# The second router's front inside the attention, and a shared expert with its inner units on the partitions

## The chip, the cores and the metric

One core of a Trainium2 chip runs the kernel. Times are microseconds on the device for one execution; the metric is the median of the runs.

## What is computed

The input is 16 images of 16 x 16 tokens of 256 channels: 4096 tokens. Two layers, each a mixing part and a mixture of experts, with residuals:

```python
x = x + L0_conv(_ln_c(x))                     # spectral mixing, the kernel's first stage
t = t + L0_ffn(_ln_t(t))                      # 8 experts, top 2
x = x + L1_conv(_ln_c(x))                     # 3x3 convolution, column and row attention with gates
t = t + L1_ffn(_ln_t(t))                      # 8 experts, top 2, and a shared one
# in L1_ffn:
logits = x @ w_router.T; probs = softmax(logits); top 2, weights divided by their sum
routed = square(relu(x @ w1[e].T)) @ w2[e].T  # e: the token's two experts
shared = square(relu(x @ ws1.T)) @ ws2.T      # 256 -> 512 -> 256, every token
return shared + routed
```

## The kernel before

The residual stream `x_res` stays in SBUF, 32 tiles of 128 tokens. Stages follow each other: mixing (0 to 85 us of the profile), first router and experts (to 535), the attention (535 to 843.1), the second router's front (to 903.7) and tail (to 940), the second experts (to 1082), the shared expert (to the end). Products are made in fp32r halves: a number is a high half (a copy in fp32r, ScalarE) and a low one (the rest, VectorE, `low_half`), and `product` (L171 to L179) is three matmuls, high x high, high x low and low x high.

**The attention** takes 8 pairs of images as a pipeline. Each engine has a list of calls, written out by hand and run in order, for steps i = -1 (ScalarE: -2) to 7 + DRAIN, DRAIN = 4: a step convolves pair i (18 convolution steps, `convolve`), makes queries, values, scores and softmax of pair i-1, the gates of pair i-2 (`gate_layer`, six small layers of fp32 between TensorE and VectorE's `leaky`), and attends along the rows, multiplies by `end_w` (`finish`) and adds pair i-3 or i-4 to `x_res`. GpSimd gathers two routed rows for each token (`y_in`), VectorE adds them (`add_routed`), sums them (`statistics`, `deviations`), ScalarE takes the root with Ln and Exp (`root`) and normalises; pair 0 is done whole before pair 1, and then the first step begins. The half of the channels from the pooled branch is added by `join`, pair by pair, in the last steps. ScalarE loads a table ahead of each Exp or Ln of another set.

**The router** (L218 to L523) has a front and a tail. The front takes images one by one: `BATCH_NORM_STATS2` of each tile, root and three Newton instructions for 8 tiles together, normalisation (half on VectorE, half on ScalarE), a store of the normalised rows to `h_rows`, four transposes (`bankT`), a copy to `xT`, and 2 fp32 products a tile with `xT` as the stationary operand and 8 columns of weights. In the same loop the second layer's weights (20 pieces of 512 columns) are loaded to a stage of four, and split (`halves`). The tail selects two experts of 8 for each token and builds the slot tables.

**The shared expert** is `mlp(..., experts=False)`: for each tile of 128 tokens, load the rows, turn them (2 transposes, L640), split, project (6 matmuls of 512 columns, L177 to L179), Relu (L720), square (L767), turn (4 transposes, L647), split, project back (12 matmuls of 256 columns), and add it and the two gathered rows of the experts. Each stage has two buffers (`RING` = 2), so tiles overlap; GpSimd gathers the routed rows (L588).

## Time and profile before

| | us |
|---|---|
| runs | 1211.38, 1213.06, 1213.83 (median 1213.06) |
| profiled execution, and its span | 1207.68, 1205.8 |
| PE busy | 1034.9 (86%) |
| PEld busy | 893.0 |
| DVE busy | 628.5 (52%) |
| ACT busy | 528.2 (44%) |
| POOL busy | 266.8 (22%) |
| mean granted TensorE clock | 0.919 of 2.4 GHz |

PE is TensorE's matmuls, PEld its weight loads, DVE is VectorE, ACT ScalarE, POOL GpSimd, and SP (SyncE) issues the DMAs. Busy shares are means over stages with different limits. PEclk is the granted clock of TensorE, 1.00 for 2.4 GHz and 0.50 for 1.2 GHz.

### The profile page before, as it was taken

What the parts mean: (1) busy time and instruction counts of PE and PEld (TensorE: products, weight loads), DVE (VectorE), ACT (ScalarE), POOL (GpSimd) and SP (SyncE); (2) the same over time, 40 slices, a digit from 0 to 9 for tenths busy, and PEclk for the clock granted to TensorE, in tenths of its full rate; (3) what the DMA queues carried; (4) which work ended last, traced back from release to release, by engine and by line L of the source; (5) the groups of instructions that cost most, each with busy time, mean ns of one, the idle gap of its engine ahead of it and who ended that gap; (6) DMA issues with size and microseconds to landing.
All of it is one profiled execution on the core that took longest, in us unless ns stands there. A gap on an engine that the chain in (4) does not pass through costs nothing. (4 is left out here: it accounts for less than half of the span.)

```text
span 1205.8 us, 20734 instructions
## 1 busy us (share of the span) xinstructions
PE 1034.9 (86%) x5905; PEld 893.0 (74%) x5905; DVE 628.5 (52%) x1686; ACT 528.2 (44%) x1333; POOL 266.8 (22%) x274
## 2 busy tenths in 40 slices
PE   6966679999999999962699999985575799989998
PEld 6955568888888888852466666664575799978997
DVE  5488653222222333225456665455758455546887
ACT  6037254444444444423354555330545566653433
POOL 0000012111111111117522000000000544525664
PEclk9999999999999999985799999975555899999999
DMA  9533501111111111126311100000630344434553
GB/s 356 228 122 123 175 27 49 54 56 54 54 53 53 53 53 53 45 102 181 92 53 53 36 1 1 1 35 1 183 131 1 111 140 138 139 114 130 156 151 107
DMA packets 65398, 110.44 MB, mean 92 GB/s; under 512 B 10068, under 2 KB 47590, under 8 KB 64295
## 3 DMA queue, kind: packets, MB, share of 16 engines
q1 hardware_dynamic: 52070, 73.46, 17.4%
q0 software_dynamic: 12960, 35.41, 10.5%
q8 instruction: 56, 0.92, 0.3%
q10 hardware_dynamic: 288, 0.47, 0.1%
q14 instruction: 24, 0.19, 0.0%
HBM read 73.90 MB, written 35.40 MB: 91 GB/s over the span
## 5 line engine op out<-in xcount | busy, mean ns | idle before, releaser
L580 POOL DMA_INDIRECT experts_rows_sb<-h_rows,ids_i x142 | 134.3, 946 | 762.6 <-POOLq L523 435.6
L767 DVE TENSOR_TENSOR experts_a_sb<-experts_a_sb,experts_bankU 128x512 f32<-128x512 f32 x71 | 48.9, 688 | 224.2 <-PE experts_bankU L179 224.2
L720 ACT ACTIVATE experts_a_sb<-experts_bankG 128x512 f32<-128x512 f32 (+1 forms) x142 | 69.7, 491 | 93.3 <-PE experts_bankG L179 91.9
L711 ACT ACTIVATE experts_hT<-experts_bankH 128x256 fp32r<-128x256 f32 x142 | 54.1, 381 | 89.7 <-PE experts_bankH L640 89.7
L733 ACT ACTIVATE experts_y_sb<-experts_bankY 128x256 f32<-128x256 f32 x142 | 54.5, 384 | 85.6 <-PE experts_bankY L176 66.8
L921 POOL DMA_INDIRECT attn_y<-y_rows,pos_i x64 | 65.1, 1018 | 103.5 <-DVE x_res L1263 50.3
L177 PE MATMUL attn_bankC<-attn_padded,attn_w_half 128*128 128x512 f32 x144 | 75.7, 526 | 6.9 <-ACT attn_feat L1156 4.6
L588 POOL DMA_INDIRECT shared_routed_sb<-y_rows,pos_i x64 | 67.2, 1050 | 62.4 <-DVE x_res L790 34.9
L176 PE MATMUL experts_bankY<-down_plain,experts_aT_plain 128*128 x284 | 72.9, 379 | 0.0
L331 PE MATMUL moe_bankT<-konst_sb,xn 128*128 128x128 f32 x128 | 34.8, 431 | 44.3 <-DVE xn L387 44.3
L182 DVE TENSOR_TENSOR experts_aT<-experts_bankA,experts_aT 128x256 fp32r<-128x256 f32 x142 | 59.6, 420 | 24.0 <-ACT experts_aT L728 24.0
L647 PE MATMUL experts_bankA<-konst_sb,experts_a_sb 128*128 128x128 f32 x426 | 69.7, 273 | 0.4 <-DVE experts_aT L182 0.4
L177 PE MATMUL experts_bankG<-gate_high,experts_hT 128*128 x142 | 69.6, 490 | 0.0
L182 DVE TENSOR_TENSOR experts_hT<-experts_bankH,experts_hT 128x256 fp32r<-128x256 f32 x142 | 59.8, 421 | 18.6 <-ACT experts_hT L711 18.6
L640 PE MATMUL experts_bankH<-konst_sb,experts_rows_sb 128*128 128x128 f32 x284 | 55.4, 277 | 16.3 <-issue 14.2
L178 PE MATMUL attn_bankC<-attn_padded,attn_w_half 128*128 128x512 f32 x144 | 62.7, 436 | 0.0
L179 PE MATMUL attn_bankC<-attn_padded,attn_w_half 128*128 128x512 f32 x144 | 62.4, 433 | 0.0
L767 DVE TENSOR_TENSOR experts_a_sb<-experts_a_sb,experts_bankG 128x256 f32<-128x256 f32 x71 | 29.9, 421 | 58.1 <-ACT experts_a_sb L720 57.4
L331 PEld LDWEIGHTS moe_bankT<-konst_sb,xn 128*128 128x128 f32 x128 | 26.0, 240 | 46.0 <-DVE xn L387 29.1
L342 PEld LDWEIGHTS moe_logits<-router_sb,moe_xT 128*128 128x128 f32 x256 | 58.2, 333 | 1.8 <-ACT moe_xT L307 1.8
L640 PEld LDWEIGHTS experts_bankH<-konst_sb,experts_rows_sb 128*128 128x128 f32 x284 | 37.3, 142 | 26.3 <-issue 17.2
L178 PE MATMUL experts_bankG<-gate_low,experts_hT 128*128 x142 | 56.6, 398 | 0.0
(348 smaller groups left out, 2958.8 us busy)
## 6 DMA issues: line engine op xcount, KB each, us to landing
y_rows<-experts_y_sb SPq DMA_DIRECT2D x142, 128.0 KB
h_rows<-xn SPq DMA_DIRECT2D x32, 256.0 KB, 3.7
x_res<-in_x SPq DMA_DIRECT2D x4, 1024.0 KB, 12.0
mix_xT<-in_xt SPq DMA_DIRECT2D x4, 1024.0 KB, 13.9
gate_raw<-in_L_ffn_gate_w SPq DMA_DIRECT2D x1, 4096.0 KB, 13.8
up_raw<-in_L_ffn_up_w SPq DMA_DIRECT2D x1, 4096.0 KB, 23.2
x_rows<-x_res SPq DMA_DIRECT2D x16, 256.0 KB, 2.4
x_res<-x_rows SPq DMA_DIRECT2D x8, 512.0 KB, 3.8
```

What stands on the lines that cost most here:

```text
L176: return nc.tensor.matmul(out, left[0], right[0], start=start, stop=stop)
L177: nc.tensor.matmul(out, left[0], right[0], start=start, stop=False)
L178: nc.tensor.matmul(out, left[0], right[1], start=False, stop=False)
L179: return nc.tensor.matmul(out, left[1], right[0], start=False, stop=stop)
L182: return eng.tensor_tensor(low, whole, high.bitcast(F32), ALU.subtract)
L580: nc.gpsimd.indirect_dma_start(rows[t % DEPTH][:, :], None, h_dram, bass.IndirectOffsetOnAxis(ap=ids_i[:, t:t + 1], axis=0)).then_inc(s_ro ...
L588: nc.gpsimd.indirect_dma_start(routed[u % DEPTH_R][:, :], None, y_dram, bass.IndirectOffsetOnAxis(ap=pos_i[:, j + k * TILES:j + k * TILES ...
L640: last = nc.tensor.transpose(bankH[:, kc * P:(kc + 1) * P], rows[i % DEPTH][:, kc * P:(kc + 1) * P], K("ident"))
L647: last = nc.tensor.transpose(bankA[:, k * P:(k + 1) * P], a_sb[i % RING][:, k * P:(k + 1) * P], K("ident"))
L720: nc.scalar.activation(a_sb[i % RING][:, :], bankG[i % RING][:, 0:hidden], ACT.Silu if gate is not None else ACT.Relu).then_inc(s["act"], 1)
L767: nc.vector.tensor_tensor(a_sb[i % RING][:, :], a_sb[i % RING][:, :], bankU[i % RING][:, 0:hidden], ALU.mult).then_inc(s["a"], 1)
L921: nc.gpsimd.indirect_dma_start(y_in[u % Y_RING][:, :], None, y_dram, bass.IndirectOffsetOnAxis(ap=pos_i[:, j + k * TILES:j + k * TILES + 1 ...
```

## The change

It has four parts. (1) The front of the second router goes into the attention: pair p's statistics run in step p+4, its transposes, copies and logits in step p+5, DRAIN is 5, the logits stay in `logits1`, the turned rows of a pair go from one buffer `xT` to a new `h_turned` in DRAM, and part 0 of the selection runs in the last step. The logits now have the 8 columns of weights as the stationary operand and 256 columns of `xT` moving, and are turned back. The weights' 20 pieces are split in the steps that `SHARES` names. (2) The attention starts with half pairs (`FIRST`, `SECOND`), convolves 12 of pair 0's 18 convolution steps before it turns pair 1, uses one table set for Ln and Exp (`preload_act_table_set`), and adds the branch in two batches (`JOINS`). (3) The second router is `router_tail` alone. (4) `shared` replaces the `mlp` of the shared expert: groups of 4 tiles, 8 in all, whose turned rows are loaded (512 KB) and split; `ws1` is the stationary operand, so the inner units come out on the partitions and nothing is turned; Relu, Square and Copy run on ScalarE.

```diff
+ht_dram = nc.dram_tensor("h_turned", (P, KC * TOKENS), F32, kind="Internal").ap()
...
-    select(dve, chain, 0)
-    counted.append(chain.n)
-front.close()
-if between is not None:
-    between()
+    dve.wait_ge(s["logits"], PARTS[0][1] // HALVES)
+    choice.select(chain, 0, logits_ps[0][:, 0:PARTS[0][1] * E])
...
+def shared(ws1, ws2):
+    GROUP = 4
+    GROUPS = TILES // GROUP
+    KI = IS // P
+    LEAD = KI + 2
+    DEPTH = 8
+    N = GROUP * P
...
+def load(g):
+    if g >= GROUPS:
+        return
+    if g >= RING:
+        sp.wait_ge(s["h_low"], g - RING + 1)
+    sp.dma_start(hT_raw[g % RING][:, :], ht_dram[:, g * KC * N:(g + 1) * KC * N]).then_inc(s_raw[g % RING], 16)
+for g in range(2 * RING):
+    load(g)
+for g in range(GROUPS):
+    load(g + 2 * RING)
+    for t in range(g * GROUP, (g + 1) * GROUP):
+        sp.wait_ge(s["added"], t + 1)
+        sp.dma_start(out[t * P:(t + 1) * P, :], x_tile(t)).then_inc(s["stored"], 16)
+sp.wait_ge(s["stored"], TILES * 16)
...
+def project(c):
+    g, k = c // KI, c % KI
+    if g >= GROUPS:
+        return
+    pe.wait_ge(s["h_low"], g + 1)
+    if g:
+        pe.wait_ge(s["relu"], c - KI + 1)
+    for kc in range(KC):
+        last = product(bankU[k][:, :], [w[:, kc * IS + k * P:kc * IS + (k + 1) * P] for w in ws1],
+                       [x[:, kc * N:(kc + 1) * N] for x in hT[g % RING]], kc == 0, kc == KC - 1)
+    last.then_inc(s["up"], 1)
+def project_back(t):
+    g = t // GROUP
+    pe.wait_ge(s["a_low"], (g + 1) * KI)
+    if t >= GROUP:
+        pe.wait_ge(s["added"], t - GROUP + 1)
+    for k in range(KI):
+        at = k * N + t % GROUP * P
+        last = product(bankY[t % GROUP][:, 0:C], [x[:, at:at + P] for x in aT[g % RING]],
+                       [w[:, k * C:(k + 1) * C] for w in ws2], k == 0, k == KI - 1)
+    last.then_inc(s["down"], 1)
+for c in range(LEAD):
+    project(c)
+for t in range(TILES):
+    project_back(t)
+    project(t + LEAD)
...
+def activate(c):
+    g, k = c // KI, c % KI
+    act.wait_ge(s["up"], c + 1)
+    if g:
+        act.wait_ge(s["a_low"], c - KI + 1)
+    nc.scalar.activation(a[k][:, :], bankU[k][:, :], ACT.Relu).then_inc(s["relu"], 1)
+    act.wait_ge(s["relu"], c + 1)
+    nc.scalar.activation(a[k][:, :], a[k][:, :], ACT.Square).then_inc(s["square"], 1)
+    act.wait_ge(s["square"], c + 1)
+    if g >= RING:
+        act.wait_ge(s["down"], (g - RING + 1) * GROUP)
+    nc.scalar.activation(aT[g % RING][0][:, k * N:(k + 1) * N], a[k][:, :], ACT.Copy).then_inc(s["a_high"], 1)
+high_h(0)
+high_h(1)
+for c in range(GROUPS * KI):
+    activate(c)
+    if c % KI == KI - 1:
+        high_h(c // KI + RING)
...
+def low_a(c):
+    g, k = c // KI, c % KI
+    if g >= GROUPS:
+        return
+    dve.wait_ge(s["a_high"], c + 1)
+    part = slice(k * N, (k + 1) * N)
+    low_half(nc.vector, aT[g % RING][1][:, part], a[k][:, :], aT[g % RING][0][:, part]).then_inc(s["a_low"], 1)
+def add_routed(t):
+    if t >= TILES:
+        return
+    for k in range(2):
+        u = t * 2 + k
+        dve.wait_ge(s_routed[u % DEPTH], (u // DEPTH + 1) * 16)
+        if k:
+            dve.wait_ge(s["sum"], u)
+        nc.vector.scalar_tensor_tensor(out=x_tile(t), in0=routed[u % DEPTH][:, :], scalar=w_top[:, t + k * TILES:t + k * TILES + 1],
+                                       in1=x_tile(t), op0=ALU.mult, op1=ALU.add).then_inc(s["sum"], 1)
+def add_y(t):
+    dve.wait_ge(s["down"], t + 1)
+    dve.wait_ge(s["sum"], t * 2 + 2)
+    nc.vector.tensor_tensor(x_tile(t), x_tile(t), bankY[t % GROUP][:, 0:C], ALU.add).then_inc(s["added"], 1)
+low_h(0)
+low_h(1)
+for c in range(LEAD):
+    low_a(c)
+    if c == KI - 1:
+        low_h(RING)
+add_routed(0)
+for t in range(TILES):
+    add_routed(t + 1)
+    add_y(t)
+    c = t + LEAD
+    low_a(c)
+    if c % KI == KI - 1:
+        low_h(c // KI + RING)
...
+SHARES = {0: 3, 1: 3, 2: 2, 8: 3, 9: 2, 10: 2, 11: 2, 12: 3}
...
+loaded = 0
+for i in range(0, PAIRS + DRAIN):
+    if has(i + 2):
+        sp.wait_ge(s["sum"], (i + 1) * 2 * PT)
+        load_x(i + 2)
+    while loaded < min(share[i].start + len(stage), len(pieces)):
+        halves.load(sp, loaded)
+        loaded = loaded + 1
+    if i in BATCH_AT:
+        b = BATCH_AT.index(i)
...
+    if has(i - 5):
+        width = KC * 512
+        sp.wait_ge(s["f_copied"], 2 * (i - 5) + 2)
+        sp.dma_start(ht_dram[:, (i - 5) * width:(i - 4) * width], xT[:, :]).then_inc(s_turned_out, 16)
+    if has(i - 4):
+        for m in range(2 * (i - 4), 2 * (i - 4) + 2):
+            sp.wait_ge(s["f_xn"], m + 1)
+            sp.dma_start(rows[:, m * HALVES:(m + 1) * HALVES, :],
+                         xn[m % RING][:, :].rearrange("p (h c) -> p h c", c=C)).then_inc(s_stored[m % RING], 16)
+for b in range(RING):
+    sp.wait_ge(s_stored[b], IMAGES // RING * 16)
+sp.wait_ge(s_turned_out, PAIRS * 16)
...
+def turn_rows(p, n):
+    if not has(p):
+        return
+    m = p * 2 + n
+    pe.wait_ge(s["f_xn"], m + 1)
+    pe.wait_ge(s["lows"], min(2 * (p + 5) + 2, IMAGES))
+    if m:
+        pe.wait_ge(s["f_copied"], m)
+    for kc in range(KC):
+        for h in range(HALVES):
+            last = nc.tensor.transpose(bankT[:, (kc * HALVES + h) * P:(kc * HALVES + h + 1) * P],
+                                       xn[n][:, h * C + kc * P:h * C + (kc + 1) * P], K("ident"))
+    last.then_inc(s["f_turned"], 1)
...
+def route(p, n, kc):
+    if not has(p):
+        return
+    pe.wait_ge(s["f_copied"], p * 2 + n + 1)
+    pe.wait_ge(s["feat2"], min(p + 3, PAIRS))
+    if p:
+        pe.wait_ge(s["f_kept"], p)
+    part = slice(n * 256, (n + 1) * 256)
+    last = nc.tensor.matmul(bankX[0:E, part], router1[:, kc * E:(kc + 1) * E], xT[:, kc * 512 + n * 256:kc * 512 + (n + 1) * 256],
+                            start=(kc == 0), stop=(kc == KC - 1))
+    if (n, kc) == (1, KC - 1):
+        last.then_inc(s["f_logits"], 1)
+def turn_logits(p):
+    if not has(p):
+        return
+    pe.wait_ge(s["f_logits_t"], p + 1)
+    for t in range(PT):
+        last = nc.tensor.transpose(bankX[:, t * E:(t + 1) * E], logits_t[:, t * P:(t + 1) * P], K("ident", E)[:, 0:E])
+    last.then_inc(s["f_turned_back"], 1)
...
-for i in range(-1, PAIRS + DRAIN):
+turn(0, 0)
+turn(0, 1)
+convolve(0, 0, 12)
+turn(1, 0)
+convolve(0, 12, STEPS)
+turn(1, 1)
+for i in range(1, PAIRS + DRAIN):
...
+turn_rows(i - 5, 0)
 gate_layer(i - 2, 1)
-convolve(i, 5, 6)
-turn(i + 1, 0)
-convolve(i, 6, 7)
+convolve(i, 5, 7)
+turn_rows(i - 5, 1)
 gate_layer(i - 2, 2)
 convolve(i, 7, 8)
 scores(i - 1, "down")
 convolve(i, 8, 9)
+turn(i + 1, 0)
+route(i - 5, 0, 0)
 gate_layer(i - 2, 3)
 convolve(i, 9, 10)
 scores(i - 1, "along")
 convolve(i, 10, 11)
+route(i - 5, 0, 1)
 gate_layer(i - 2, 4)
+route(i - 5, 1, 0)
 convolve(i, 11, 12)
+turn_values(i - 1)
+route(i - 5, 1, 1)
+convolve(i, 12, 13)
+branch(i)
+gate_layer(i - 2, 5)
+convolve(i, 13, 14)
 turn(i + 1, 1)
-turn_values(i - 1)
-convolve(i, 12, 13)
-gate_layer(i - 2, 5)
-branch(i)
-convolve(i, 13, 14)
 turn_probs(i - 1, "down")
+turn_logits(i - 5)
...
+def roots(p, f, tiles=WHOLE):
+    cols = slice(tiles[0], tiles[-1] + 1)
+    if has(p):
+        act.wait_ge(s["var"], batch(p, tiles) + 1)
+        nc.scalar.activation(m_log[:, cols], m_var[:, cols], ACT.Ln).then_inc(s["log"], 1)
+    if has(f):
+        act.wait_ge(s["f_var"], f + 1)
+        nc.scalar.activation(f_log[:, :], f_var[:, :], ACT.Ln).then_inc(s["f_log"], 1)
+    if has(p):
+        act.wait_ge(s["log"], batch(p, tiles) + 1)
+        nc.scalar.activation(m_rstd[:, cols], m_log[:, cols], ACT.Exp, scale=-0.5).then_inc(s["root"], 1)
+    if has(f):
+        act.wait_ge(s["f_log"], f + 1)
+        nc.scalar.activation(f_rstd[:, :], f_log[:, :], ACT.Exp, scale=-0.5).then_inc(s["f_root"], 1)
...
+def copy_rows(p, n):
+    if not has(p):
+        return
+    act.wait_ge(s["f_turned"], p * 2 + n + 1)
+    if p:
+        act.wait_ge(s["f_logits"], p)
+        act.wait_ge(s_turned_out, p * 16)
+    nc.scalar.activation(xT[:, :].rearrange("p (k x) -> p k x", k=KC)[:, :, n * 256:(n + 1) * 256],
+                         bankT[:, :].rearrange("p (k x) -> p k x", k=KC), ACT.Copy).then_inc(s["f_copied"], 1)
+def copy_logits(p):
+    if not has(p):
+        return
+    act.wait_ge(s["f_logits"], p + 1)
+    nc.scalar.activation(logits_t[:, :], bankX[0:E, :], ACT.Copy).then_inc(s["f_logits_t"], 1)
...
+nc.scalar.preload_act_table_set("natural_log_exp_and_others")
 act.wait_ge(loads["conv"], 16)
 for n in range(W_PARTS):
     nc.scalar.activation(w_half[0][:, w_part(n)], w_raw[:, w_part(n)], ACT.Copy).then_inc(s["w_high"], 1)
-nc.scalar.activation(warm[:, :], K("ones")[:, 0:4], ACT.Ln)
 act.wait_ge(s["border"], 1)
-for i in range(-2, PAIRS + DRAIN):
+for n, half in enumerate((FIRST, SECOND)):
+    roots(0, PAIRS, half)
+    normalise(0, half)
+    high(0, n)
+roots(1, PAIRS)
+normalise(1)
+for i in range(0, PAIRS + DRAIN):
     if i == 1:
         act.wait_ge(loads["attn"], ATTN_LOADS * 16)
     relu(i - 1)
     copy_feat2(i - 3)
     queries(i - 1)
+    copy_rows(i - 5, 0)
+    copy_rows(i - 5, 1)
     high(i + 1, 0)
     exponentials(i - 1, "down")
     exponentials(i - 1, "along")
+    if i > PAIRS + 2:
+        roots(i + 2, i - 4)
+    copy_logits(i - 5)
+    values(i - 1)
+    gate_exp(i - 2)
+    if i <= PAIRS + 2:
+        roots(i + 2, i - 4)
     high(i + 1, 1)
-    values(i - 1)
-    root(i + 2)
-    gate_exp(i - 2)
     copy_along(i - 1)
     copy_gated(i - 2)
     normalise(i + 2)
-    relu_branch(i)
+    for piece in share[i]:
+        halves.high(act, piece)
...
+def normalise_rows(p):
+    if not has(p):
+        return
+    dve.wait_ge(s["f_root"], p + 1)
+    chain(nc.vector.tensor_tensor(f_newton[:, :], f_var[:, :], f_rstd[:, :], ALU.mult))
+    chain(nc.vector.tensor_tensor(f_newton[:, :], f_newton[:, :], f_rstd[:, :], ALU.mult))
+    chain(nc.vector.tensor_scalar(f_newton[:, :], f_newton[:, :], -0.5, 1.5, ALU.mult, ALU.add))
+    chain(nc.vector.tensor_tensor(f_scale[:, :], f_rstd[:, :], f_newton[:, :], ALU.mult))
+    chain(nc.vector.tensor_tensor(f_bias[:, :], f_mean[:, :], f_scale[:, :], ALU.mult))
+    for n in range(2):
+        if p:
+            dve.wait_ge(s["f_turned"], p * 2 + n - 1)
+            dve.wait_ge(s_stored[n], p * 16)
+        for h in range(HALVES):
+            t = n * HALVES + h
+            last = nc.vector.tensor_scalar(xn[n][:, h * C:(h + 1) * C], x_tile(p * PT + t), f_scale[:, t:t + 1], f_bias[:, t:t + 1],
+                                           ALU.mult, ALU.add)
+        last.then_inc(s["f_xn"], 1)
+def keep_logits(p):
+    if not has(p):
+        return
+    dve.wait_ge(s["f_turned_back"], p + 1)
+    last = nc.vector.tensor_copy(logits1[:, p * PT * E:(p + 1) * PT * E], bankX[:, 0:PT * E])
+    last.then_inc(s["f_kept"], 1)
...
-add_routed(0, 0, range(PT))
-for t in range(PT):
-    low_weights(t)
-    add_routed(0, 1, range(t, t + 1))
-statistics(0)
-deviations(0)
+for k in range(2):
+    add_routed(0, k, FIRST)
+statistics(0, FIRST)
+low_weights(0)
+add_routed(0, 0, SECOND[0:1])
+deviations(0, FIRST)
+add_routed(0, 0, SECOND[1:2])
+low_weights(1)
+low_weights(2)
+add_routed(0, 1, SECOND[0:1])
+low_weights(3)
+add_routed(0, 1, SECOND[1:2])
+statistics(0, SECOND)
 lows(0, 0)
+deviations(0, SECOND)
+add_routed(1, 0, WHOLE)
 lows(0, 1)
-for k in range(2):
-    add_routed(1, k, range(PT))
+add_routed(1, 1, WHOLE)
 statistics(1)
 deviations(1)
 tables()
+JOINS = {(4, 0): (0,), (4, 1): (1, 2), (5, 1): (3,), (8, 0): (4,), (8, 1): (5,), (9, 1): (6, 7)}
 for i in range(0, PAIRS + DRAIN):
     sum_rows(i - 2)
     sum_columns(i - 3)
     add(i - 4)
+    if i == PAIRS + DRAIN - 1:
+        choice.select(chain, 0, logits1[:, 0:PARTS[0][1] * E])
     add_routed(i + 2, 0, range(0, PT // 2))
     leaky(i - 2, 0)
+    for p in JOINS.get((i, 0), ()):
+        join(p)
+    row_stats(i - 4, 0)
     add_routed(i + 2, 0, range(PT // 2, PT))
     leaky(i - 2, 1)
-    lows(i + 1, 0)
+    row_stats(i - 4, 1)
     add_routed(i + 2, 1, range(0, PT // 2))
     leaky(i - 2, 2)
+    row_stats(i - 4, 2)
     add_routed(i + 2, 1, range(PT // 2, PT))
-    join(2 * (i - PAIRS))
     maximum(i - 1, "down")
     leaky(i - 2, 3)
+    row_stats(i - 4, 3)
+    lows(i + 1, 0)
     statistics(i + 2)
-    join(2 * (i - PAIRS) + 1)
     maximum(i - 1, "along")
     leaky(i - 2, 4)
+    row_variances(i - 4)
     soften(i - 1, "down")
-    lows(i + 1, 1)
     soften(i - 1, "along")
+    relu_branch(i)
     bound(i - 2)
     copy_down(i - 1)
     sigmoid(i - 2)
+    if i <= PAIRS + 2:
+        keep_logits(i - 5)
     apply_rows(i - 2)
+    lows(i + 1, 1)
     apply_columns(i - 3)
     deviations(i + 2)
+    if i >= PAIRS:
+        normalise_rows(i - 4)
     copy_attended(i - 1)
+    if i < PAIRS:
+        normalise_rows(i - 4)
+    for p in JOINS.get((i, 1), ()):
+        join(p)
+    for piece in share[i]:
+        halves.low(dve, piece)
+    if i > PAIRS + 2:
+        keep_logits(i - 5)
...
-mlp("shared", TILES, IS, ws1, ws2, experts=False, sink=out)
...
+with routing:
+    router_tail("moe1", choice, logits1[:, PARTS[1][0] * E:PARTS[1][1] * E])
+mlp("experts1", SLOT_TILES, I1, up1, down1)
+shared(ws1, ws2)
```

Not shown: `row_stats` and `row_variances` are `BATCH_NORM_STATS2` of one tile, and the small sums from them; `high_h` and `low_h` split a group's h as ScalarE's copy (one instruction of 1024 columns) and VectorE's rest; both `row_` functions run in the step that adds the pair.

## Rows read from the trace of the kernel before

**Rows 1.** Windows by stage: busy us (count) of PE, PEld, DVE, ACT, POOL; PEclk, DMA, GB/s.
```profile
535.00:563.80 28.80, 2.20 (x8) 1.43 (x8) 13.34 (x45) 10.27 (x18) 21.82 (x21) 0.50 0.68 218
563.80:596.50 32.70, 19.24 (x63) 14.32 (x63) 19.52 (x70) 10.81 (x20) 21.13 (x20) 0.76 0.36 109
596.50:792.50 196.00, 190.08 (x929) 129.56 (x929) 109.44 (x325) 92.30 (x250) 22.17 (x24) 0.99 0.09 26
792.50:843.10 50.60, 34.26 (x151) 26.00 (x150) 27.14 (x80) 10.55 (x32) 0.00 (x0) 0.62 0.05 20
843.10:903.70 60.60, 40.85 (x192) 39.74 (x192) 40.19 (x133) 29.68 (x58) 0.00 (x0) 0.50 0.49 156
903.70:940.00 36.30, 18.57 (x76) 16.99 (x76) 25.36 (x79) 17.25 (x66) 3.78 (x4) 0.50 0.05 15
940.00:1082.00 142.00, 137.85 (x1135) 135.75 (x1134) 77.58 (x213) 94.02 (x284) 63.29 (x67) 0.99 0.42 129
1082.00:1205.80 123.80, 114.97 (x768) 103.10 (x768) 94.55 (x192) 44.17 (x96) 67.20 (x64) 0.97 0.47 137
```

**Rows 2.** Timeline of DVE, end of the attention to the selection: start us, busy us.
```profile
841.71 1.42 DVE L1401 TENSOR_TENSOR x_res<-x_res,attn_branches 128x256 f32<-128x256 f32 x4
844.36 0.75 DVE L360 BATCH_NORM_STATS2 stats<-x_res 128x6 f32<-128x256 f32 x2 [1.24 <-PEq L120]
...
903.66 0.23 DVE L256 TENSOR_REDUCE moe_top<-moe_logits 128x8 f32<-128x64 f32 x1 [3.76 <-PEq L407]
```

**Rows 3.** Timeline of PE in one tile of the shared expert.
```profile
1153.13 0.40 PE L177 MATMUL shared_bankG<-ws,shared_hT 128*128 128x512 f32 x1
...
1154.53 0.38 PE L640 MATMUL shared_bankH<-konst_sb,shared_rows_sb 128*128 128x128 f32 x2
1154.74 0.60 PE L647 MATMUL shared_bankA<-konst_sb,shared_a_sb 128*128 128x128 f32 x4
1155.10 0.36 PE L177 MATMUL shared_bankY<-ws,shared_aT 128*128 128x256 f32 x1
...
1156.61 0.40 PE L177 MATMUL shared_bankG<-ws,shared_hT 128*128 128x512 f32 x1
```

**Rows 4.** Groups of instructions by line: busy us, mean ns of one, idle before.
```profile
L588 POOL DMA_INDIRECT shared_routed_sb<-y_rows,pos_i x64 | 67.2, 1050 | 62.4 <-DVE x_res L790 34.9 <-POOLq L535 16.8 <-issue 10.7
L720 ACT ACTIVATE shared_a_sb<-shared_bankG 128x512 f32<-128x512 f32 x32 | 19.1, 598 | 65.1 <-PE shared_bankG L179 62.9 <-issue 2.2
```

**Rows 5.** Timeline of PE in a full step: its final product, an fp32 product.
```profile
736.35 1.16 PE L1072 MATMUL attn_bankS_along<-end_w,attn_gated 128*128 128x128 f32 x8
...
740.29 1.07 PE L965 MATMUL attn_bankQ<-attn_feat,qk_w 128*64 128x512 f32 x2
```

**Rows 6.** Timeline of ACT and PE in one full step of the attention.
```profile
728.75 1.28 ACT L1138 ACT_TABLE_LOAD   x1
...
731.99 0.66 PE L1043 MATMUL attn_bankX<-konst_sb,attn_gated 128*128 128x128 f32 x4 [0.80 <-DVE attn_gated L1373]
```

**Rows 7.** Timeline of PE at the attention's start.
```profile
580.87 1.12 PE L937 MATMUL attn_bankT<-konst_sb,attn_xn 128*128 128x128 f32 x4 [10.19 <-ACT attn_xn L1128]
```

**Rows 8.** Timeline of DVE in the second router's front.
```profile
848.50 0.17 DVE L375 TENSOR_TENSOR newton<-var_eps,rstd 128x8 f32<-128x8 f32 x1
...
849.52 0.73 DVE L387 TENSOR_SCALAR xn<-x_res,rstds,moe_shift 128x256 f32<-128x256 f32 x2
```

**Rows 9.** Timeline of PE: the final products of steps 8 to 11.
```profile
792.97 1.16 PE L1072 MATMUL attn_bankS_along<-end_w,attn_gated 128*128 128x128 f32 x8
...
814.49 1.16 PE L1072 MATMUL attn_bankS_along<-end_w,attn_gated 128*128 128x128 f32 x8
...
828.03 2.08 PE L1072 MATMUL attn_bankS_along<-end_w,attn_gated 128*128 128x128 f32 x8
...
838.99 2.08 PE L1072 MATMUL attn_bankS_along<-end_w,attn_gated 128*128 128x128 f32 x8
```

**Rows 10.** Timeline of PE: a group of transposes in the drain.
```profile
805.99 1.12 PE L1001 MATMUL attn_bankQ<-konst_sb,attn_exp_down 128*128 128x128 f32 x4
```

465 lines of the change are left out of this document (275 added, 190 removed).

## The prediction

> **What bounds the kernel now.** I read the windows by stage first [rows 1]. The attention's steps keep TensorE busy (190 of 196 us at clock 0.99), and so do the second experts (138 of 142 us) and the shared expert (115 of 124 us). Three stretches are bound by chains between engines: the attention's start (535 to 596.5 us), its drain (792.5 to 843.1 us, clock 0.62) and the second router's front (843.1 to 903.7 us, clock 0.50, TensorE and VectorE both two thirds busy). The front is serial: it begins when the last join has ended, and the tail begins after it [rows 2]. The shared expert's token tile was read from the timeline [rows 3]: six products of 512 columns take 1.40 us, the two transposes of h 0.21 us, the four of a 0.36 us, twelve products of 256 columns 1.51 us, 3.48 us in all with no gap. The remaining rows are the prices of what moves and the waits near it.
>
> **The front leaves.** From the last join's end (843.13 us) to the tail's first instruction (903.66 us) lie 60.5 us; the same barrier that now stands between 843.13 and 844.36 us stays [rows 2]. So 59.3 us go, before what comes back.
>
> **What comes back in the full steps (i = 5 to 7).** TensorE gets, for each pair of images, 8 transposes, 4 fp32 products of 256 columns and 4 small transposes of the logits. Four transposes cost 0.36 us [rows 3]; an fp32 product of 512 columns runs in two passes of 1.07 us together [rows 5], so one of 256 about 0.5 us; the small ones I put at 0.1 each (between nothing, hidden, and the 0.09 of a full transpose plus a start). That is 0.7 + 2.0 + 0.5 = 3.2 us a step, and TensorE has no idle time to put it in: a step of 28.3 us (two of them from 736.35 to 792.97 us, [rows 5, 9]) has one gap of 0.8 us [rows 6]. The second group of transposes waits for ScalarE's copy of the first, which stands behind five activations of the queries: 0.7 us more. VectorE gets about 6.5 us a step: 4 statistics (0.35 each, [rows 2]), small sums (0.9), five chained small ones (1.0) and four normalisations (0.35 each, [rows 8]), a join. VectorE is busy 109 of 196 us [rows 1], 16 of 28 us a step, so its share fits, but the normalisations (2.5 us) stand behind the copy of the attended values and in front of the sums of rows and columns, for which the next step's first gate layer waits on TensorE, and behind that layer the queries, values and everything else. The slack there is about 1 us, so 1.9, 1.2 and 0.5 us with the joins, 3.6 in all. Sum for three steps: 3 x 3.9 + 3.6, rounded to +16 us. Bounds: +8 if the VectorE work is hidden, +25 if each added VectorE microsecond after the copy reaches TensorE.
>
> The weight halves (20 pieces of 512 columns, 0.6 us each on ScalarE [rows 4] and, as two 256-column pieces, 0.7 on VectorE [rows 2]) are split over steps 0 to 2 (8 pieces) and 8 to 12 (12). In steps 0 to 2 they stand just ahead of the relu that frees the convolution's bank, 0.6 us each on ScalarE: +5 us (bounds 0 and +8).
>
> **Table loads.** Each step loads two activation tables ahead of the gate's exponential; one load is 1.28 us, and TensorE then waits 0.8 us for the gated values [rows 6]. With logarithm and exponential in one set both loads go: 7 x 0.8, about -5 us (bounds 0 and -6; nothing if the set is not kept). The Trainium skill (ScalarE: Activation LUTs, Table sets: the hidden batching unit) says the same of that set, and under What ACT_TABLE_LOAD costs it adds a drain, 2.66 us a switch. The trace has the next activation right behind the 1.28 us; by the page's figure the loads would be worth twice as much to ScalarE, and the sum would still end at the 0.8 us gaps.
>
> **The attention's start.** Now the gathers of four tiles, two each, must land before the first statistics; the second pair's convolution operands come so late that TensorE waits 10.2 us at 580.87 us [rows 7], and step 1 starts at 596.5 us. The change takes the first half pair's tokens as soon as its own four gathers are in, fills TensorE with 12 of 18 convolution steps before it turns the next pair, and takes its table loads off. Following the queues with the durations of this stretch, the first convolution starts near 559 instead of 563.8 us and step 1 near 584: -12 us. Bounds: 0, if the next gathers set the pace (GpSimd issued gathers for 21.8 of the first 28.8 us, [rows 1]), and -16.
>
> **The drain.** Before, from one final product to the next, steps 8 to 10 take 21.5, 13.5 and 11.0 us, and 4.1 us are left to the end [rows 9]: with what lies ahead of the first, 50.6 us [rows 1]. Now steps 8 to 10 carry the router's work of pairs 3 to 5, and 11 and 12 that of pairs 6 and 7. At half clock four transposes take 0.95 to 1.12 us [rows 10], the four products 4 us, the logits' turn 0.9: nearly 7 us of TensorE a step, laid between gate layers that wait about 0.5 us each on VectorE. I take +5 for step 8 and +4.5 each for 9 and 10. Step 11 grows from 5 to about 11: behind the final product and addition come statistics, roots and normalisation of pair 7 (8 us), while TensorE works through pair 6. Step 12 is new, a bare chain: turn, copy, turn, copy, four products, copy, turn back, copy, with three weight halves in front of the last copy, about 10 us. Sum 14 + 6 + 10 = +30 us. Bounds: +18 (clock 2.4 GHz, the halves hidden) and +45 (each step as long as its VectorE and TensorE work end to end).
>
> **The shared expert.** Six transposes a tile go: 0.57 us x 32 = 18.2 us [rows 3]. TensorE stays the bound if the others fit in 2.91 us: ScalarE runs three dependent 512-column activations of 0.6 us a tile [rows 4] and a quarter of a 1024-column one, 2.1 us, or 2.5 if each hand-over costs 0.15; VectorE about 2.3 (94.6 us over 32 tiles [rows 1], less the 0.7 of the squaring); GpSimd two gathers of 1.05 plus 0.3 between them [rows 4], 2.7 us. The start is some 4 us later (512 KB to load and split instead of 128 KB, four chunks before the first product back), but six projections are done by then, and after the last product one addition stands instead of three. I take -18. Bounds -12 (ScalarE or gathers at 3.1 us a tile) and -20.
>
> **Sum**: -59.3 + 16 + 5 - 5 - 12 + 30 - 18 = -43 us on the profiled execution's 1207.7 us: 1164 us. The median of the runs is 5.4 us above that execution, so 1170 us.
>
> **Rivals.**
> A, the clock. The drain is at half clock because TensorE is idle a third of it [rows 1]; the added work could hold 2.4 GHz. Then its 7 us a step halve, five times 3.5 us, of which about 12 lie on the chain: 1158 us. For it: the drain begins at full clock; against it: the front did much the same work, two thirds busy, at 0.50 throughout [rows 1]. Chance 0.13. The Trainium skill (TensorE: Matmul & The Clock Gate, What's actually happening) ties the clock to how busy the engine has recently been, which speaks for A; what was added is a third transposes, which Part 4: PE-mode transpose says do not count as busy.
> B, the start gains nothing: gathers set its pace. 1182 us. For it: GpSimd's share there; against it: TensorE's long wait ends on normalised rows, not on a gather. 0.14.
> C, the shared expert becomes ScalarE's or GpSimd's: 1176 us. ScalarE was busy only 44 of 124 us, but its work is now chained. 0.07.
> D, the front is moved but not hidden: VectorE becomes the bound of steps 4 to 7 and of the drain, both terms at their upper bounds (+9 and +15). 1194 us. 0.07.
> E, slower than before: one buffer holds the turned rows, and the copy of a pair waits until the store of the pair before has landed; the store waits in SyncE's queue behind weight loads that wait for VectorE. If each of 8 pairs waited over 43/8 = 5.4 us for it, the gain is gone; at 7 us a pair it would be 1170 + 56 = 1226 us. A store of such a size lands in about 4 us after its issue and steps are 11 us or longer, so there is slack. 0.04.
>
> **Chances.** Forecast 0.55. What a measurement of this kernel can tell from no change is about 0.2%. All but E are faster: 0.95, with 0.01 within 0.2% and 0.04 slower. The range takes in A, B, C and the near side of D, and the terms' bounds where only one or two fail together: 1150 to 1192 us.
>
> **What would show it.** Right: no stage between the attention's last step and the router's selection, the tail starting near 878 us (903.7 - 59.3 + 16 + 5 - 5 - 12 + 30); steps 5 to 7 some 4 to 5 us longer; the 10.2 us wait gone; fewer than three table loads in the attention; shared tiles 2.9 us apart with TensorE busy. Wrong: gaps on TensorE in front of the first gate layer above 3 us a step, a drain over 95 us, waits on ScalarE's chain or on gathers in the shared expert, or SyncE holding the turned rows. The numbers fail most easily in the drain, which is worked out from durations, not read.

## The result, and the profile after

The changed kernel took 1196.28 us (median of 4 runs, 1192.82 to 1199.71), the kernel before 1212.22 beside it: ratio 0.9882, 95% interval 0.986 to 0.9905. It is faster, as forecast, but by 16 us instead of 43, and lies above the range of 1150 to 1192 us. Its windows by stage, cut at the same places as before [rows 1]; the columns are the same:

```profile
535.00:601.90 66.90, 23.21 (x70) 15.73 (x70) 34.46 (x125) 16.49 (x37) 39.82 (x40) 0.60 0.50 157
601.90:785.90 184.00, 174.79 (x837) 117.09 (x837) 116.84 (x374) 77.75 (x230) 24.04 (x24) 0.97 0.17 55
785.90:898.70 112.80, 93.50 (x408) 58.22 (x407) 69.90 (x235) 37.86 (x98) 0.00 (x0) 0.74 0.23 80
898.70:935.00 36.30, 18.54 (x76) 17.00 (x76) 25.39 (x79) 16.15 (x65) 3.79 (x4) 0.50 0.05 15
935.00:1078.00 143.00, 139.13 (x1135) 136.62 (x1134) 77.72 (x213) 94.23 (x284) 63.45 (x67) 0.98 0.42 128
1078.00:1197.30 119.30, 99.63 (x576) 87.58 (x576) 69.85 (x136) 65.70 (x104) 65.38 (x64) 0.90 0.47 142
```

The tail starts at 898.7 us where 878 was forecast, and the shared expert takes 119.3 us where some 106 were. Both shortfalls have a place. First the attention's start, timeline of TensorE, with the idle time before an instruction and its releaser in brackets:

```profile
572.92 0.42 PE L180 MATMUL attn_bankC<-attn_padded,attn_w_low 128*128 128x512 f32 x1
...
576.24 0.56 PE L178 MATMUL attn_bankC<-attn_padded,attn_w_high 128*128 128x512 f32 x1 [2.13 <-issue]
578.38 0.59 PE L179 MATMUL attn_bankC<-attn_padded,attn_w_high 128*128 128x512 f32 x1 [1.58 <-issue]
580.48 0.58 PE L180 MATMUL attn_bankC<-attn_padded,attn_w_low 128*128 128x512 f32 x1 [1.51 <-issue]
...
601.93 0.77 PE L178 MATMUL attn_bankC<-attn_padded,attn_w_high 128*128 128x512 f32 x1 [8.73 <-ACT attn_feat L1432]
```

The three matmuls from 576.24 to 580.48 us are of one product, wait for nothing in the program, and begin 2.1 us apart instead of 0.26. In the same microseconds VectorE and ScalarE stand still (timelines of the two):

```profile
576.25 0.41 DVE L183 TENSOR_TENSOR attn_bias_part<-attn_bias_raw,attn_bias_part 2x256 fp32r<-2x256 f32 x1 [7.11 <-issue]
...
589.92 0.66 ACT L1423 ACTIVATE attn_padded<-attn_bankT 128x256 fp32r<-128x256 f32 x2 [20.12 <-remote]
```

VectorE's instruction follows the one before it on its own engine. The transposes for which ScalarE would wait here ended at 572.56 us. I call such a stretch a stall. Two more lie in the shared expert; the first of them, timeline of TensorE:

```profile
1111.34 0.40 PE L179 MATMUL shared_bankU<-shared_hT,ws 128*128 128x512 f32 x1
1112.25 0.40 PE L180 MATMUL shared_bankU<-shared_hT,ws 128*128 128x512 f32 x1 [0.51 <-issue]
1114.34 0.39 PE L178 MATMUL shared_bankU<-shared_hT,ws 128*128 128x512 f32 x1 [1.69 <-issue]
1115.09 0.39 PE L179 MATMUL shared_bankU<-shared_hT,ws 128*128 128x512 f32 x1 [0.36 <-issue]
```

### The profile page after: what moved, and what is told of

It reads as the page before. It is cut to its first block and busy times, and to the rows that moved or that the text cites. A ratio compares the mean times of both kernels' runs of the same rounds, so it can differ in the third digit from the quotient of the medians.

```text
span 1197.3 us, 19835 instructions
## 1 busy us (share of the span) xinstructions
PE 1025.8 (86%) x5686; PEld 858.5 (72%) x5686; DVE 615.7 (51%) x1712; ACT 528.2 (44%) x1328; POOL 264.1 (22%) x274
## 5 line engine op out<-in xcount | busy, mean ns | idle before, releaser
L178 PE MATMUL attn_bankC<-attn_padded,attn_w_high 128*128 128x512 f32 x144 | 76.4, 530 | 19.8 <-ACT attn_feat L1432 14.6
L834 POOL DMA_INDIRECT shared_y<-y_rows,pos_i x64 | 65.4, 1022 | 63.9 <-DVE x_res L943 32.1
L178 PE MATMUL experts_bankG<-gate_high,experts_hT 128*128 x142 | 69.6, 490 | 0.0
L180 PE MATMUL attn_bankC<-attn_padded,attn_w_low 128*128 128x512 f32 x144 | 63.8, 443 | 1.5 <-issue 1.5
L179 PE MATMUL attn_bankC<-attn_padded,attn_w_high 128*128 128x512 f32 x144 | 63.6, 442 | 1.6 <-issue 1.6
L179 PE MATMUL experts_bankG<-gate_low,experts_hT 128*128 x142 | 56.6, 398 | 0.0
L178 PEld LDWEIGHTS attn_bankC<-attn_padded,attn_w_high 128*128 128x128 f32 x144 | 28.7, 199 | 38.3 <-issue 32.9
L180 PE MATMUL experts_bankG<-gate_high,experts_hT 128*128 x142 | 55.7, 392 | 0.0
L180 PE MATMUL experts_bankU<-up_high,experts_hT 128*128 x142 | 55.5, 391 | 0.0
## 6 DMA issues: line engine op xcount, KB each, us to landing
mix_xT<-in_xt SPq DMA_DIRECT2D x4, 1024.0 KB, 14.1
```

Source lines behind the costliest of these rows:

```text
L178: nc.tensor.matmul(out, left[0], right[0], start=start, stop=False)
L179: nc.tensor.matmul(out, left[0], right[1], start=False, stop=False)
L180: return nc.tensor.matmul(out, left[1], right[0], start=False, stop=stop)
L834: nc.gpsimd.indirect_dma_start(routed[u % DEPTH][:, :], None, y_dram, bass.IndirectOffsetOnAxis(ap=pos_i[:, t + k * TILES:t + k * TILES + ...
```

## The experiments

Eighteen more runs, some of them the same kernel again, were made in five more sets; the kernels of a set run on one chip and share the runs of the kernel before. That one took 1199.46 us in set 2 and 1209.64, 1210.71, 1211.72 and 1210.17 in sets 3 to 6, against 1212.22 in the first. So set 2 differs from the others, and ratios are compared within a kind. The chip is not the difference: sets 2 and 6 ran on the same one.

**again** (set 2): the changed kernel, no edit.

> The changed kernel, nothing altered. In its first trace the tail starts at 898.7 us, 20 us later than forecast, and the shared expert takes 119.3 us, 14 longer than forecast. Most of it lies in three stretches where several engines start their instructions one or two microseconds apart with no releaser in the trace: 569 to 590 us in the attention's start, 1110 to 1118 and 1154 to 1158 in the shared expert. Theory 1: these stalls belong to the changed program (its instructions, or the transfers around them): the second trace has them at the same instructions with the same length, and the ratio to the kernel before is again 0.986 to 0.990. Theory 2: they come and go with the execution: the trace has them elsewhere or not at all, step 1 of the attention begins near 584 us instead of 601.9, and the span differs by over 5 us.

Measured: 1166.88 us against 1199.46, ratio 0.9722 (0.9702 to 0.9743). Its windows, cut at the same instructions:

```profile
535.00:582.90 47.90, 19.09 (x71) 14.09 (x71) 33.85 (x123) 16.00 (x37) 36.98 (x36) 0.68 0.64 203
582.90:766.30 183.40, 174.32 (x837) 117.44 (x837) 116.91 (x374) 77.41 (x230) 28.03 (x29) 0.97 0.19 59
766.30:877.80 111.50, 91.97 (x408) 57.64 (x407) 69.97 (x236) 37.73 (x98) 0.00 (x0) 0.75 0.24 81
877.80:914.00 36.20, 18.48 (x76) 16.99 (x76) 25.36 (x79) 16.05 (x65) 3.78 (x4) 0.50 0.05 15
914.00:1057.00 143.00, 139.05 (x1135) 136.62 (x1134) 77.72 (x213) 94.36 (x284) 63.30 (x67) 0.97 0.42 128
1057.00:1162.20 105.20, 92.69 (x576) 83.04 (x576) 70.10 (x136) 66.51 (x104) 67.47 (x64) 0.94 0.53 161
```

Row by row the two traces agree within 1.3 us, except in the first (19.0 us shorter) and the last (14.1 us shorter), where the stalls lie. So it is theory 2: the stalls come and go, by sets. ScalarE's copy that stood 20 us comes 1.6 us after the transposes:

```profile
570.09 0.67 ACT L1423 ACTIVATE attn_padded<-attn_bankT 128x256 fp32r<-128x256 f32 x2 [2.34 <-PE attn_bankT L1154]
```

The two traces differ in a second way. Here is the same wait of TensorE in the changed kernel's first trace and in this one:

```profile
556.97 1.12 PE L1154 MATMUL attn_bankT<-konst_sb,attn_xn 128*128 128x128 f32 x4 [5.91 <-issue]
```
```profile
554.96 1.12 PE L1154 MATMUL attn_bankT<-konst_sb,attn_xn 128*128 128x128 f32 x4 [5.89 <-ACT attn_xn L1397]
```

It is an ordinary wait for ScalarE, and as long in both; the first trace merely names no releaser for it. Counted from the traces, both hold 19835 instructions, but the first holds 9118 records of semaphores being raised and this one 12988. All 20 traces of this case hold 4229 to 4253 of them up to 520 us. Behind that the three traces of set 2 hold 8743 to 9168 more, and the 17 others 4855 to 5749. So "no releaser" is no sign of a stall in a trace of the other sets; a stall is told by instructions that wait for nothing and yet stand apart. And every trace with stalls has lost records too, so the recording itself, or what hinders both, is a rival for their cause. No run tests it: each execution on record was profiled.

**start_old** (set 2) and again in set 6: the start of the kernel before.

```diff
-                convolve(0, 0, 12); turn(1, 0); convolve(0, 12, STEPS); turn(1, 1)
+                convolve(0, 0, 6); turn(1, 0); convolve(0, 6, 12); turn(1, 1); convolve(0, 12, STEPS)
-                for n, half in enumerate((FIRST, SECOND)): ...
+                roots(0, PAIRS); normalise(0); high(0, 0); high(0, 1)
```

> The attention's start of the kernel before (pair 0 whole, its order of gathers, pair 1 turned after 6 and 12 of 18 convolution steps), all else as changed. Theory 1, the new start is worth what I forecast and the stall at 569 to 590 us hides it: with the old start step 1 begins near 596 us less the table loads (3 us), so 593 to 597, some 5 to 8 us earlier than in the changed kernel's trace, ratio to before about 0.982 to 0.985. Theory 2, the stall has nothing to do with the order: it is there too, step 1 begins at 605 us or later, ratio 0.992 or more.

> The attention's start of the kernel before in the otherwise changed kernel, in another set of executions. Without stalls it was 4.0 us slower (1170.8 against 1166.9). With stalls the kernel before lost 10 to 13 us there and the changed kernel 17 to 20; if that belongs to the order of the start, this kernel is 2 to 5 us faster than the changed kernel's 0.988 (0.984 to 0.986); if it does not, 4 us slower (0.991).

Measured: set 2, 1170.84 us, ratio 0.9753 (0.9732 to 0.9775), 4.0 us slower than the changed kernel, and no run of one overlaps the other's; step 1 begins at 587.57 instead of 582.89 us. Set 2 has no stall, so neither of the first two theories was put to the test. Set 6: 0.9861 (0.9833 to 0.9889), about 2 us faster than the changed kernel's 0.988 of other sets, less than the intervals; its start loses 9 us to the stall by the two traces, where the changed kernel's loses 19. So the new start is worth 4 us, and the stalls take it back. start_old keeps the table set: its first convolution begins 26.9 us after the stage's first instruction, 28.7 in the kernel before, so the loads left out are worth 1.8 us more up to there. TensorE's wait for the second pair's rows, 10.2 us in the kernel before [rows 7], is this in set 2:

```profile
572.36 0.66 PE L1152 MATMUL attn_bankT<-konst_sb,attn_xn 128*128 128x128 f32 x4 [2.41 <-ACT attn_xn L1396]
```

**shared_old** (set 2) and again in set 6: the shared expert before.

```diff
-        shared(ws1, ws2)
+        mlp("shared", TILES, IS, ws1, ws2, experts=False, sink=out)
```

> The shared expert of the kernel before, as a loop with transposes, all else as changed (the turned rows are still stored, and not read). Theory 1, the new shared expert saves 4 to 5 us as the two traces say (123.8 against 119.3): ratio to before 0.991 to 0.993. Theory 2, in most executions the stalls in it are shorter and it saves the 18 us forecast: ratio about 1.002.

> The shared expert of the kernel before in the otherwise changed kernel, in another set of executions. In a set without stalls it was 18.1 us slower than the changed kernel (1185.0 against 1166.9). In a set with stalls the changed shared expert loses 12 to 14 us to them and this one, by the traces of the kernel before, nothing: 4 to 9 us slower than the changed kernel's 0.988, so 0.991 to 0.995.

Measured: set 2, 1184.99 us, ratio 0.9875 (0.9852 to 0.9898), 18.1 us slower than the changed kernel. Set 6: 0.995 (0.9925 to 0.9975), which is 8 to 9 us slower. The new shared expert saves the 18 us forecast where nothing stalls, and half of that elsewhere. The old one is slower with stalls too, by less: from its first matmul to the end it takes 119.4 us in set 2, 123.4 in set 6, and 121.5 to 123.0 in the three traces of the kernel before.

**before_again** (set 3) and **before_third** (set 4): the kernel before, no edit.

> The kernel before, nothing altered. The runs beside the last kernels gave it 1199.5 us, 12.7 us less than beside the first run of the changed kernel, and its first trace has VectorE's small dependent instructions 1.3 us apart between 569 and 582 us, where the rest of the trace has them 0.2 apart. If that stretch is the same stall as in the changed kernel's first trace, this trace has it not, the first convolution of step 1 begins 9 to 12 us earlier (585 to 588 us instead of 596.5), and the span is near 1195. If the 12.7 us lie elsewhere, step 1 begins at 596 us again.

> The kernel before, nothing altered, for a trace without the stall. Its first two traces have it in the attention's start (VectorE's dependent instructions 1.3 us apart at 569 to 582 us) and took 1207.7 and 1208.2 us. Either the executions of this set are of the kind that gave 1199.5 us: then step 1's convolution begins at 585 to 588 us and nothing else moves by more than 1 us; or they are of the other kind, with 596 us again.

Measured: 1208.2 and 1211.54 us, step 1 at 595.96 and 597.70 us: both of the kind with stalls, so no trace of the kernel before without them exists and the test that before_again was for did not take place. The place is visible in its first trace, timeline of VectorE in the attention's start:

```profile
573.76 0.16 DVE L1289 TENSOR_TENSOR attn_newton<-attn_newton,attn_rstd 128x4 f32<-128x4 f32 x1
575.24 0.17 DVE L1290 TENSOR_SCALAR attn_newton<-attn_newton 128x4 f32<-128x4 f32 x1 [1.32 <-DVE attn_newton L1289]
576.64 0.16 DVE L1291 TENSOR_TENSOR attn_scale<-attn_rstd,attn_newton 128x4 f32<-128x4 f32 x1 [1.23 <-DVE attn_newton L1290]
```

The same three instructions follow each other in 0.2 us elsewhere. It is this chain that TensorE's wait of 10.2 us [rows 7] hangs on. With the same order of the start and no stall it was 2.4 us (start_old, set 2), so 7.8 of the 10.2 us are the stall's, less what the table loads cost there.

**no_set** (set 3) and **no_set_again** (set 4): without the table set.

```diff
-                nc.scalar.preload_act_table_set("natural_log_exp_and_others")
```

> The changed kernel without the one line that names a table set holding both logarithm and exponential: each root loads two tables again. My sum gave the loads 5 us (7 x 0.8). If that is right, the ratio to before is about 0.976 (0.9722 of the unaltered changed kernel and 5 us of 1199). The rival, ScalarE's loads are hidden because TensorE has other work there now (the waits of 0.8 us for the gated values are gone from the changed kernel's steps, 0.6 us in three places): within 1.5 us of the changed kernel, 0.972 to 0.9735, except in the drain.

> The changed kernel without the shared table set, once more, since its first runs had stalls in other places than the changed kernel and cannot be set beside it. In a set without stalls: ratio 0.976 if the loads cost the 5 us of my sum, 0.972 to 0.9735 if they are hidden; steps 5 to 7 then take 34.1, 33.2 and 32.0 us with or without them.

Measured: ratios 0.9957 (0.9931 to 0.9984) and 0.9979 (0.9959 to 0.9998), 9 to 12 us slower than the changed kernel's 0.988 in such sets. In the second trace step 1 begins at 597.42 and the tail at 905.0 us, 307.6 us; the changed kernel has 601.93 and 898.7, 296.8. So 10.8 us of it lie behind the start, in two traces of different sets, neither of which has a stall there. Steps 1 to 5 take 7.1 us of them (157.9 against 150.8), with five pairs of loads that the kernel before has there as well; the other 3.7 us belong to six pairs of later steps, all for the router's roots, which the kernel before takes in its front. So 1.4 us a pair where I priced 0.8: both my 5 us and the rival's nothing fall. In no_set's trace step 1 takes 33.2 us instead of the 30.8 of no_set_again, and VectorE stands 12.7 us in it, up to 603.12; so a stall lies behind its start, and I take no price from it.

**spread** (set 3): the first 8 weight pieces one a step.

```diff
-            SHARES = {0: 3, 1: 3, 2: 2, 8: 3, ...}
+            SHARES = {0: 1, 1: 1, 2: 1, 3: 1, 4: 1, 5: 1, 6: 1, 7: 1, 8: 3, ...}
```

> The first 8 of the 20 weight pieces are split one a step in steps 0 to 7 instead of 3, 3 and 2 in steps 0 to 2. TensorE waits 7.7, 3.3 and 2.0 us for the relu ahead of the convolutions of steps 1 to 3 in the changed kernel; 0.56 us of ScalarE a piece lies in front of each. If the copies in front of the relu are the cause of these waits, they shrink by 1.1 to 1.7 us each and no new wait of over 0.5 us comes in steps 4 to 8: 2 to 4 us faster than the changed kernel (ratio 0.969 to 0.9705). If each piece costs its 0.56 us wherever it stands, no difference (0.972).

Measured: 0.9880 (0.9848 to 0.9913), as the changed kernel. Steps 1 to 3 take 83.9 us instead of 87.9, but steps 4 to 7 take 130.4 instead of 128.1 and step 8 takes 31.1 instead of 29.0: what steps 1 to 3 gain, the others lose, so a piece costs its half microsecond wherever it stands.

**split** (set 3): group 0 of the shared expert in halves.

```diff
+                        if g == 0:
+                            for kc in range(KC):
+                                sp.dma_start(hT_raw[0][:, kc * N:(kc + 1) * N], ...)   # copy and low half too
```

> Group 0 of the shared expert loaded, copied and split in two halves of 256 KB. TensorE waits 8.5 us at the stage's start for a load, a copy of 1.04 and a low half of 1.23 us one after the other. With halves the first product needs half of each: 1.1 us less of the two engines and up to 1 us less of the load, so 1 to 2 us faster than the changed kernel (ratio 0.9705 to 0.9715); none if ScalarE's chain of relu, square and copy behind the first chunks is what sets the pace.

Measured: 0.9875 (0.985 to 0.99). TensorE's wait at the start falls from 8.5 to 6.7 us, and 1.2 us of it come back ahead of the first product back. Inconclusive in time.

**best** (set 4): `split`, and the late pieces in steps 8 to 10.

```diff
-            SHARES = {0: 3, 1: 3, 2: 2, 8: 3, 9: 2, 10: 2, 11: 2, 12: 3}
+            SHARES = {0: 3, 1: 3, 2: 2, 8: 4, 9: 4, 10: 4}
```

> The changed kernel with two alterations: the last 12 weight pieces are split in steps 8, 9 and 10 (4 each) and none in steps 11 and 12, and group 0 of the shared expert is loaded and split in halves. I forecast three halves in front of step 12's last copy as part of its 10 us. If they lie on that chain, the stretch from the last final product to the tail (18.0 us in the trace without stalls) shrinks by 1.5 to 3 us, while steps 8 to 10, where ScalarE is busy 12 of 28, 5 of 19 and 3 of 14 us, grow by less than 1; with 1 to 2 us for the halves 2.5 to 4 us faster than the changed kernel, ratio 0.969 where that has 0.972. If it waits for the engines' other work, no difference.

Measured: 0.9901 (0.9872 to 0.993), no gain. From the last final product to the tail 17.4 us instead of 18.9, but steps 6, 9 and 10 grow by 1.5, 1.2 and 1.2 us and only step 8 shrinks, by 1.7.

**unroll** (set 4): the old shared expert, its loops written out.

```diff
+                    if not experts:
+                        for t in range(AHEAD, n_tiles):
+                            step(t, (t - AHEAD) % DEPTH + AHEAD, ahead=t + AHEAD < n_tiles)
+                        return
...
-                        with sp.Fori(2, n_tiles // DEPTH) as q:
+                        for q in range(2, n_tiles // DEPTH):
```

> The changed kernel with the shared expert of the kernel before, ScalarE's, VectorE's and SyncE's loops written out (TensorE's list was written out already). Theory S, the stalls belong to stretches in which all engines run code that is written out: in a set of executions with stalls this shared expert has them as well, 5 to 12 us, and takes 128 to 136 us; in a set without, 124 us as the loop. Theory R, they belong to the new shared expert's own transfers or waits: 124 us in either set.

Measured: 0.9953 (0.9931 to 0.9974); the stage takes 124.7 us (1074.7 to 1199.4) with no idle time of TensorE over 1 us without a releaser, while the start of the same trace stalls (577 to 590 us). From its first matmul it takes 122.7 us, the loop 121.5 to 123.4 in such sets. Written-out code alone does not bring the stall; theory S falls.

**again_second**, **no_gathers**, **no_loads**, **light** (set 5, with stalls): what the stalls need.

```diff
# no_gathers
-                    for t in range(TILES):        # GpSimd, shared expert
+                    for t in range(0):
...
-            SHARES = {0: 3, 1: 3, 2: 2, 8: 3, 9: 2, 10: 2, 11: 2, 12: 3}
+            SHARES = {3: 3, 4: 3, 5: 2, 8: 3, 9: 2, 10: 2, 11: 2, 12: 3}
# no_loads
-                        if g >= GROUPS:           # loads of turned rows
+                        if g >= RING:
...
+                    if p == 2:                    # GpSimd, attention
+                        pool.wait_ge(s["conv"], 1)
# light, and the convolution of pair 0 likewise
-                            last = product(bankU[k][:, :], [... for w in ws1], [... for x in hT[g % RING]], ...)
+                            last = product(bankU[k][:, :], [... for w in ws1[:1]], [... for x in hT[g % RING][:1]], ...)
```

> The changed kernel, nothing altered, beside the next three kernels. Three of four sets of executions so far had the stalls (the kernel before 1208 to 1212 us, the changed one and its near relatives 1193 to 1200) and one had none (1199.5 and 1166.9). With stalls: 569 to 590 us, 1111 to 1120 and 1154 to 1162 us, some 35 us in all against the trace without, ratio 0.985 to 0.990. Without: ratio 0.972.

> Leaves out the shared expert's gathers and the addition of the routed rows; and in the attention the weight pieces are loaded from step 2 on and split in steps 3 to 5 instead of 0 to 2. Theory G, the stalls come with GpSimd's gathers or with the weight loads behind them: TensorE has no idle times of over 1 us without a releaser in the shared expert, and the first stall, 573 to 590 us, is gone or moved behind the weight loads. Theory N, transfers have no part in it: both stalls at the same instructions, 4 to 8 us each.

> Leaves out the loads of turned rows from group 2 on (groups 2 to 7 compute with the rows of groups 0 and 1); and in the attention's start the gathers of pair 2 wait until the convolution of pair 0 is done. Theory L, the stalls come with the 512 KB loads that are under way when they begin (issued 2 us before the stall at 1112 us): none in the shared expert. Theory G for the start: none at 573 to 590 us, where now no gather is issued. Theory N: both as before.

> Leaves out two of three products (high with low, low with high) in the shared expert and in the convolution of pair 0, so TensorE works a third of the time there. Theory P, the stalls follow a stretch of TensorE at full rate (it was busy all of 1095 to 1111 and 1120 to 1153 us before them): neither stall comes. Theory N: TensorE's list is shorter, but where ScalarE and VectorE are in the same code they stall 4 to 17 us as before, and the shared expert, then bound by ScalarE at some 2 us a tile, 64 to 75 us, has one or two gaps of this kind.

Measured: again_second 0.9876 (0.9848 to 0.9904), stalls at 574 to 590, 1117 to 1121, 1157 to 1171 us. no_loads 1.0009: its shared expert stalls without the loads (118.2 us). In the attention its gathers pause from 557 to 576 us, and where the changed kernel stalls TensorE, VectorE and ScalarE keep their spacing. The stall comes later, timeline of ScalarE:

```profile
571.61 0.66 ACT L1423 ACTIVATE attn_padded<-attn_bankT 128x256 fp32r<-128x256 f32 x2 [2.86 <-PE attn_bankT L1154]
...
618.84 0.56 ACT L1458 ACTIVATE attn_q_down<-attn_bankQ,qk_sb 16x256 f32<-16x256 f32 x1 [19.20 <-remote]
```

The first line is the copy that stood 20 us in the changed kernel. The second had its operand at 605.5 us, when the queries' product ended, and starts 2 us after the last of 32 gathers that GpSimd issued without a pause from 576.48 to 616.8 us.

The other two: light 0.9778: with a third of the matmuls VectorE still stands 8.2 us ahead of 576.3 us, and falls behind its times in the trace of again by 6.9 and 8.8 us, at 1106 to 1117 and 1141 to 1152 us. no_gathers 0.9724: the start stalls (574 to 585 us), the shared expert does not. Its window (first row, with the stage's 102.5 us) and the changed kernel's without stalls, two traces:

```profile
1067.00:1169.50 102.50, 93.17 (x576) 83.39 (x576) 42.93 (x72) 66.52 (x104) 0.00 (x0) 0.95 0.26 83
```
```profile
1085.00:1150.00 65.00, 65.00 (x420) 58.97 (x419) 49.89 (x100) 46.85 (x74) 50.69 (x48) 1.00 0.57 168
```

So the stalls need gathers in the shared expert (none without them, one kernel), and in the start they moved when the gathers did (one kernel, in which nothing else of the start was changed). They need neither the large loads, nor the weight loads of the start, which no_gathers had moved away, nor TensorE at full rate. The rest of the time that no_loads lost I put down to its own pause.

**paced** (set 6): the gathers held back to the tile that needs them.

```diff
                                 pool.wait_ge(s["sum"], u - DEPTH + 1)
+                                pool.wait_ge(s["down"], t - 3)
```

> The changed kernel, with the shared expert's gathers for tile t issued only when tile t-4 has its product back: two gathers a tile, as in the loop before. In the changed kernel they come in rows of 8 to 12, 1.25 us apart, when VectorE has caught up. Without gathers the shared expert had no stall in a set that had them elsewhere. Theory B, the rows of gathers bring the stalls: in a set with stalls none in the shared expert, which takes 105 to 109 us instead of 117 to 119, ratio near 0.978; in a set without, no difference (0.972). Theory C, any gathers do: 115 to 119 us, ratio 0.988 as the changed kernel.

Measured: 0.9842 (0.9807 to 0.9878), some 4 us faster than the changed kernel's 0.988 of other sets, a difference that the intervals leave uncertain; the stage takes 112.6 us, and TensorE has no idle time over 1 us without a releaser behind its first product. The edit did not give two gathers a tile: GpSimd still issues rows of 6 to 8, 1.25 us apart, with 1.9 to 2.4 us between them, where the changed kernel has rows of 8 to 12. With rows somewhat shorter, half of the stage's loss of 14 us is gone in the one trace. That lies between theory B and theory C and decides for neither.

```profile
1079.00:1191.60 112.60, 96.62 (x576) 83.52 (x576) 69.24 (x136) 64.91 (x104) 61.99 (x64) 0.94 0.50 150
```

## Why the prediction was wrong, point by point

The steps can be read in the trace without stalls (again). That execution took 1163.99 us, and its tail starts at 877.8 us: the sum said 1164 for the profiled execution and 878. That the sum was met there is luck in part: it was taken from a kernel before with a stall in it. In the recorded pair of traces two terms are off. The start is 5.4 us longer (step 1 at 601.93 against 596.50) where -12 was forecast, and the shared expert 4.5 us shorter (119.3 against 123.8) where -18 was: 31 of the 36 us between 1164 and 1199.71.

**The kernel before was not what its row said.** "TensorE waits 10.2 us at 580.87 us" [rows 7] I took for the kernel's own wait and booked its removal in "-12 us" for the start. Most of it was a stall: without one, the same start waits 2.4 us (start_old), and the new start, undone, is worth 4.0 us. This is the failed step of the sum: the start's term, 12 forecast, 4 measured without stalls (6 with the table loads ahead of the first convolution) and 5.4 the other way with them. Step 1 at 582.89 us (584 forecast) was right for the wrong difference. Where there is no stall the kernel before takes 12.7 us less (1199.46 against 1212.22): up to 8.9 of them lie ahead of step 1 (596.50 against 587.57), and 2 to 4 in the shared expert. Without stalls the change gives 32.6 us, 2.7%, where I forecast 43: the start lacks 6 to 8 and steps 1 to 7 take 3 too many (798.32 less 582.89 is 215.4, against 196.5 before and +16 forecast).

**The changed kernel stalls more, and no rival held that.** 19 us in the start and 14 in the shared expert, 33 of the 35 us between its two traces. This is why the recorded result lies above the range: the sum holds no term for it, and neither the shared expert's -18 nor the start's bound of 0 allows for it. Rival B, the start gains nothing, has the right sign for the recorded result, not its mechanism: gathers there are issued every 1.25 us in both traces.

**The front leaves, full steps, drain.** Final products in the trace without stalls, timeline of TensorE:

```profile
733.10 1.16 PE L1328 MATMUL attn_bankS_along<-end_w,attn_gated 128*128 128x128 f32 x8
...
798.32 1.16 PE L1328 MATMUL attn_bankS_along<-end_w,attn_gated 128*128 128x128 f32 x8
...
826.28 1.16 PE L1328 MATMUL attn_bankS_along<-end_w,attn_gated 128*128 128x128 f32 x8
...
845.37 2.08 PE L1328 MATMUL attn_bankS_along<-end_w,attn_gated 128*128 128x128 f32 x8
...
859.83 2.08 PE L1328 MATMUL attn_bankS_along<-end_w,attn_gated 128*128 128x128 f32 x8
```

Steps 6 and 7 take 65.2 us against 56.6 [rows 5, 9], 4.3 each (5.3 forecast; 3 x 3.9 + 3.6 is 15.3, which was put at 16). Steps 8 to 10 take 28.0, 19.1 and 14.5 us against 21.5, 13.5 and 11.0 [rows 9]: +6.5, +5.6, +3.5, 15.6 where 14 were forecast. Steps 11 and 12, 859.83 to 877.8, take 18.0 against 4.1, +13.9 (16 forecast). The drain as a whole +29.3, forecast +30. Behind the last copy the logits did wait for a half, timeline of VectorE:

```profile
874.40 1.90 DVE L183 TENSOR_TENSOR ws<-w_stage,ws 128x512 fp32r<-128x512 f32 x3 [0.58 <-ACT ws L213]
876.21 0.18 DVE L1759 COPY moe_logits<-attn_bankX 128x32 f32<-128x32 f32 x1
```

Rival A, the clock, falls: over the drain it was 0.61 before and 0.65 after without stalls, so for the most part still 1.2 GHz, and the chain kept its length. The two windows, before and after:

```profile
792.97:843.13 50.16, 33.79 (x150) 25.81 (x149) 27.17 (x80) 10.20 (x31) 0.00 (x0) 0.61 0.04 17
```

```profile
798.32:877.80 79.48, 60.26 (x250) 37.18 (x249) 55.02 (x186) 26.63 (x66) 0.00 (x0) 0.65 0.27 93
```

Rival E: TensorE waited 0.9 us in all, three times, for copies of turned rows in steps 1 to 8.

**Table loads.** -5 forecast; by the trace of no_set_again 7.1 us in steps 1 to 5 alone, outside my bound of 6, and 10.8 with those that the moved roots would have brought. The sum hid it: with weight halves at +5, steps 1 to 3 were to come out some 3 us longer, and are 5.4 us longer (87.3 us against the 81.9 between 596.50 and 678.36 us), so other work of those steps costs more than I booked. I priced the loads by one wait of TensorE, 0.8 us; steps 1 to 3 alone grow by 4.8 us without the set (92.7 against 87.9). The Trainium skill (ScalarE: Activation LUTs, What ACT_TABLE_LOAD costs) gives 2.66 us for a switch with its drain, about twice the row's 1.28. No row here shows that drain, and the 1.4 us a pair on TensorE's path do not tell the two apart.

**The shared expert.** -18 forecast, -18.1 measured without stalls. From 1085 to 1150 us TensorE is busy all 65.0 us at clock 1.00, and a tile takes 2.81 us (project back from 1125.57 to the next at 1128.38; 2.91 forecast). Rival C falls. ScalarE has 19.2 us of waiting for TensorE in front of its relu:

```profile
L903 ACT ACTIVATE shared_a<-shared_bankU 128x512 f32<-128x512 f32 x32 | 19.0, 595 | 19.2 <-PE shared_bankU L180 19.2
```

**Range and median.** The median was to be 5.4 us above the profiled execution. For the changed kernel it was 3.4 us below it in the first set (1196.28 and 1199.71) and 2.9 above it in set 2, so this offset is not a constant of the kernel. In the first set it happened to help: by the profiled execution the sum was 36 us short, by the median the range missed by 4 us.

## What to carry to other kernels

Small dependent instructions that suddenly stand 1.3 us apart are not a price of the kernel: look for the same instructions elsewhere in the trace, and take their spacing there before you book the removal of the wait as a gain. Do not go by a missing releaser: where the trace has lost semaphore records, many ordinary waits show none either, so compare the same wait in two traces. Price a change by parts in one set of runs, since the same kernel differed by 2.5% between sets and its ratio to the kernel before by 1.6%.

## What the runs showed of the hardware

**Stalls.** In the traces of five of six sets, TensorE, VectorE and ScalarE stood or began instructions 0.7 to 3.5 us apart for 4 to 23 us, and in the sixth never. Two traces of the changed kernel have the first stall at the same instructions of VectorE and ScalarE; in no_set it lies elsewhere. The starts keep a beat that the engines share. This is the first stall of the changed kernel, weight loads (PEld) with it:

```profile
576.97 0.28 PEld L179 LDWEIGHTS attn_bankC<-attn_padded,attn_w_high 128*128 128x128 f32 x1 [1.94 <-issue]
...
577.67 0.34 DVE L1775 TENSOR_SCALAR attn_bias_raw<-attn_bias_part,konst_sb 2x256 f32<-2x256 f32 x1 [1.01 <-DVE attn_bias_part L183]
578.38 0.59 PE L179 MATMUL attn_bankC<-attn_padded,attn_w_high 128*128 128x512 f32 x1 [1.58 <-issue]
579.07 0.47 DVE L1776 SCALAR_TENSOR_TENSOR attn_bias_rows<-attn_bias_part,konst_sb,attn_bias_raw 2x256 fp32r<-2x256 f32 x1 [1.06 <-DVE attn_bias_raw L1775]
...
579.76 0.29 PEld L180 LDWEIGHTS attn_bankC<-attn_padded,attn_w_low 128*128 128x128 f32 x1 [2.51 <-issue]
580.48 0.58 PE L180 MATMUL attn_bankC<-attn_padded,attn_w_low 128*128 128x512 f32 x1 [1.51 <-issue]
```

Until 580.48 us one of the two engines begins something every 0.70 us; VectorE's additions from 579.48 us and GpSimd's gathers, left out here, do not keep the beat. VectorE's chain in the kernel before stands 1.48 and 1.40 us apart, about twice that. That something which the engines share serves them one after the other would fit; no run shows it.

In the shared expert the stalls went with the gathers: none without them, and 2 to 4 us instead of 12 to 14 in the old shared expert, which issues two and rests 0.8 to 1.8 us. In the attention's start they moved when the gathers were held back. They set in after 9 to 30 gathers issued without a pause, and TensorE came back soon after GpSimd had to pause: it stops at 578.4 us and TensorE is back at 581.9; at 1116.6 and VectorE and ScalarE are back at 1118.0; in no_loads at 616.8 and ScalarE at 618.8. That is not a rule: in the first of these stalls ScalarE stood until 589.92 us, though GpSimd had been issuing again since 581.4. In the set without stalls GpSimd issued 48 and 56 in a row. Why that set had none stays open, and so do what a gather and the other engines share and whether the stalls would be there without the profiler's recording, which lost records in every trace that has them.

Transfers do not pile up in the stalls; the queues of the changed kernel's first trace between 565 and 600 us, packets, MB and share of 16 engines' time:

```profile
q0 software_dynamic: 950, 2.58, 25.5%
q1 hardware_dynamic: 143, 0.52, 3.9%
```

No instruction packet is among them. The Trainium skill (Runtime: NRT & Kernel Launch, Instruction fetch mechanics) has engines fetch the next 16 KiB while they execute, mostly hidden. The trace shows no fetch in its first stall, and its 16 KiB fetches behind 540 us took 1.15 us each in the mean against 1.11 in the trace without stalls; unroll, with more code written out, had none in its shared expert; so a fetch was not shown to be the cause, nor excluded.
